# Moving most of the cosine similarities, and the first batch's load of them, out of the handover between the two parts of a one-core decoder kernel

## The reference, cut to what matters

```
sim = stack([cos(embedding, emb_l), cos(embedding, embedding), cos(embedding, emb_r)], axis=1)   # [B, 3, D]
att = repeat(sim, C, axis=1)                  # [B, 3*C, D]
out = einsum('bit,oi->bot', inp_unf * att, w_flat)
```

## Time and profile before

| what | value |
|---|---|
| median of 3 runs | 1395.09 us (1395.02 to 1397.9) |
| the profiled execution's own time | 1392.16 us |
| its span, first to last instruction | 1390.1 us |
| mean granted TensorE clock | 0.992 of full |
| TensorE busy | 1355.7 us, 98% of the span |
| VectorE, ACT, POOL busy | 79%, 67%, 70% |

### The profile page before, as it was taken

The page is one execution under the profiler, slowest core; times in us unless marked ns, Lnnn a source line. Parts: engine busy times, 40 slices in busy tenths (PEclk is TensorE's granted clock), DMA queues, the critical chain, the costliest instruction groups (busy, mean ns, idle before and its releaser), DMA issues. The chain is left out here.

```text
span 1390.1 us, 32350 instructions
## 1 busy us (share of the span) xinstructions
PE 1355.7 (98%) x8306; PEld 1056.5 (76%) x8306; DVE 1095.9 (79%) x3873; ACT 927.2 (67%) x3262; POOL 979.0 (70%) x932
## 2 busy tenths in 40 slices
PE   8999999999999999999986999999999999999996
PEld 6777777777777777777764788888888888888884
DVE  6877787878778777878785688878887788877877
ACT  5887878878888887878785455545554455545544
POOL 4877777777777776777775677667776677767762
PEclk9999999999999999999998999999999999999999
DMA  7354545445453545445468866676665766666652
GB/s 266 100 160 116 159 116 161 121 146 149 121 161 115 165 115 152 132 134 159 131 201 242 185 159 166 157 174 153 161 156 164 172 152 165 156 169 157 161 122 76
DMA packets 109005, 213.03 MB, mean 153 GB/s; under 512 B 26656, under 2 KB 32288, under 8 KB 108960
## 3 DMA queue, kind: packets, MB, share of 16 engines
q1 hardware_dynamic: 108336, 211.46, 56.5%
q10 hardware_dynamic: 624, 1.05, 0.2%
HBM read 131.83 MB, written 34.47 MB: 120 GB/s over the span
## 5 line engine op out<-in xcount | busy, mean ns | idle before, releaser
L483 PE MATMUL wo_ps<-weights,halves 128*128 128x512 f32 x2304 | 569.7, 399 | 3.0 <-DVE weights L685 2.9
L483 PEld LDWEIGHTS wo_ps<-weights,halves 128*128 128x128 f32 x2304 | 421.5, 188 | 138.0 <-issue 53.3
L769 ACT ACTIVATE pexp<-sm,smin 128x128 f32<-128x128 f32 x1024 | 398.1, 391 | 100.6 <-DVE smin L622 99.7
L1197 PE MATMUL wo_ps<-weights,halves 128*128 128x512 f32 x1464 | 368.2, 399 | 4.3 <-PEq L145 4.3
L915 POOL TENSOR_TENSOR pn<-pexp,prec 128x512 f32<-128x512 f32 x256 | 266.7, 1047 | 98.5 <-DVE prec L629 98.5
L1667 POOL TENSOR_TENSOR prods<-prod,prods 128x512 fp32r<-128x512 f32 x186 | 251.6, 1360 | 119.9 <-ACT prods L1528 114.9
L1197 PEld LDWEIGHTS wo_ps<-weights,halves 128*128 128x128 f32 x1464 | 270.3, 189 | 62.6 <-issue 5.2
L622 DVE CUSTOM_DVE_ANT_0 sm<-s_ps,mask_t 128x128 f32<-128x128 f32 x1024 | 231.9, 282 | 26.1 <-PE s_ps L513 20.9
L1528 ACT CAST prods<-prod 128x512 fp32r<-128x512 f32 x189 | 117.1, 620 | 181.0 <-DVE prod L1380 146.7
L769 ACT ACTIVATION_READ_ACCUMULATOR pexp<-sm,smin 128x1 f32 x1024 | 193.0, 189 | 0.0
L1380 DVE TENSOR_TENSOR prod<-att,x 128x512 f32<-128x512 f32 x189 | 185.1, 993 | 9.5 <-DMA att<-sim_scratch 7.2
(11 more groups left out here) (130 smaller groups left out, 1645.8 us busy)
## 6 DMA issues: line engine op xcount, KB each, us to landing
att<-sim_scratch SPq DMA_DIRECT2D x192, 252.0 KB
pt<-blocks SPq DMA_DIRECT2D x636, 64.0 KB, 2.0
ctx_t<-in_ctx SPq DMA_DIRECT2D x32, 576.0 KB, 5.1
raw<-in_xT SPq DMA_DIRECT2D x32, 512.0 KB, 3.8
xn<-in_x SPq DMA_DIRECT2D x32, 512.0 KB, 7.6
ot_scratch<-ot SPq DMA_DIRECT2D x63, 256.0 KB, 2.1
raw<-ot_scratch SPq DMA_DIRECT2D x31, 512.0 KB, 6.8
out<-late SPq DMA_DIRECT2D x31, 512.0 KB, 6.2
```

Of the source, the lines that this page charges most:

```text
L483: mm = pe.matmul(qkv_ps[(par + g) % 2][:], xs[:, par, xl, k], w_sb[:, wl, g, k], start=(k == 0 and n == 0), stop=(k == KT - 1 and n == 2))
L769: ins = nc.scalar.activation(pexp[:, c % 2, i * P:(i + 1) * P], sm[:, c % 2, i * P:(i + 1) * P], ACT.Exp, bias=smin[:, c % 2, i:i + 1], sc ...
L1197: mm = pe.matmul(wo_ps[n][:], os_t[:, par, ol, k], wo_sb[:, wl, k, n * BANK:(n + 1) * BANK], start=(k == 0 and m == 0), stop=(k == KT - 1 ...
```

## The change

Similarities of the first 24 batches are made during steps 24 to 29, and only those of the last 8 at the end of part one.

- SP loads the sums of batches 0 to 23 at the start of step 24 (`load_sums(False)`); VectorE applies the limit at position 5 of step 24, ACT takes the root there, VectorE inverts in two halves in steps 25 and 26 and multiplies in steps 27 and 28, and SP stores five transfers of results in step 29. They work in 96 partitions of `att`, which is otherwise idle in part one.
- The sums of batches 24 to 31 take the old way through 32 partitions. Their stores are all issued by SP, and part two waits for them only in step 1 (own row) and step 4 (the others). The unit of the old stores on ACT's queue is gone.
- `start_att` for batch 0 loads all 1024 columns at once, on one semaphore. SP issues it in step 33 right behind the last moves of probabilities, ahead of the store of batch 31's first half and the late stores. `multiply` of batch 0 waits for all of it before its first product; part two's `load_att(0, 1)` is gone.
- Batch 31's first half goes through `ot_first`, the later columns of `xn0`, so its read waits for `added0` and not for an earlier store. Part one does not wait at its end for that store to land; part two does, in step 1, before it loads `x[2]` into `xn0`.
- Batch 0's averages, power and shift (`average_first`, `invert_root_first`) and the high and low parts of the third batch (`high_out(2)`, `low_third_out`, the latter on VectorE and not on POOL) are made at the end of part one.
- TAIL of part one goes from 4 to 10: steps 24 to 29 are unrolled, and the loop covers 4 to 23.

```diff
-    LEAD, TAIL = 4, 4
+    LEAD, TAIL = 4, 10
+    FIRST = 3 * B // 4
+    EARLY = B - 8
...
+    ot_first = xn0[:, BANK:D]
+    def sim_parts(late):
+        rows = slice(4 * FIRST, P) if late else slice(0, 4 * FIRST)
+        flat = nb if late else att[:].rearrange("p k d -> p (k d)")
...
+            if at_step(t, EARLY):
+                load_sums(False)
             if at_step(t, B):
-                load_sums()
+                load_sums(True)
...
             if at_step(t, LAST):
-                store_sims()
-                store_first_half(b)
                 sp.wait_ge(own_out, 16)
                 sp.wait_ge(sim_out, 16 * 6)
-                start_att(sp, att, att_in, sim_dram, 0, 0)
+                start_att(sp, att, att_in[0], sim_dram, 0, 0, D)
+                store_first_half(b)
+                store_sims(True)
...
+            if at_step(t, EARLY + 5):
+                store_sims(False)
...
-        sp.wait_ge(ot_out[0], 16 * B)
         sp.wait_ge(ot_out[1], 16 * (B - 1))
...
+                if at_step(t, EARLY) and p == 5:
+                    bound_sums(False)
+                if at_step(t, EARLY + 1) and p == 5:
+                    invert_norms(False, 0, HALF_QD)
+                if at_step(t, EARLY + 2) and p == 5:
+                    invert_norms(False, HALF_QD, QD + 1)
+                if at_step(t, EARLY + 3) and p == 5:
+                    pair_norms(False)
+                if at_step(t, EARLY + 4) and p == 5:
+                    cosines(False)
...
             if at_step(t, LAST):
-                invert_norms()
-                cosines()
                 add_first(1)
+                average_first()
+                invert_norms(True, 0, HALF_QD)
+                invert_norms(True, HALF_QD, QD + 1)
+                pair_norms(True)
+                cosines(True)
+                low_third_out()
...
                 if p == 7 and at_step(t, LAST):
-                    store_sims()
                     read_ot(b, 0)
                     high_later(9)
                     load_fourth_o()
+                    high_out(2)
+                if p == 5 and at_step(t, EARLY):
+                    take_root(False)
...
             if at_step(t, LAST):
                 low_out(1, 1)
+                invert_root_first()
                 low_later(9)
...
-        load_att(0, 1)
...
             if at_step(t, 4):
-                for u in range(NU):
-                    sp.wait_ge(ot_out[u], 16 * B)
+                sp.wait_ge(ot_out[1], 16 * B)
+                sp.wait_ge(sim_out, 16 * 10)
+            if at_step(t, 1):
+                sp.wait_ge(own_out, 16 * 2)
+                sp.wait_ge(ot_out[0], 16 * B)
...
-            if k == 0:
-                wait(dve, att_in[h], after(t, 64, 64))
+            if m == 0:
+                wait(dve, att_in[0], after(t, 64, 64))
+            elif k == 0:
+                wait(dve, att_in[1], after(t, 64, 0))
```

More of the change, by code:

```diff
@@ L287, in part1 @@
     QD = D // 4
-    sqs, nbs, norm = nb[:, 0:QD + 1], nb[:, QD + 1:2 * QD + 1], nb[:, 2 * QD + 1:3 * QD + 2]
-    own = rot1[:, 0, 0:QD]
-    own_out = sem("own_out")
+    HALF_QD = QD // 2
     right, ot_last = kept
+    ot_first = xn0[:, BANK:D]
+    def sim_parts(late):
+        rows = slice(4 * FIRST, P) if late else slice(0, 4 * FIRST)
+        flat = nb if late else att[:].rearrange("p k d -> p (k d)")
+        sums, mults, norm = (flat[rows, n * (QD + 1):n * (QD + 1) + width]
+                             for n, width in enumerate((QD + 1, QD, QD + 1)))
+        pair = (right[rows, :], xn0[rows, 0:QD]) if late else (
+            flat[rows, 3 * (QD + 1):3 * (QD + 1) + QD], flat[rows, 4 * (QD + 1):4 * (QD + 1) + QD])
+        return sums, mults, norm, *pair
     @block.sync
@@ L368, in load_third_o, with load_sums @@
             sp.dma_start(raw[:, 0], ot_dram[2]).then_inc(o_in[0], 16)
[L370 to L375, removed]
+        def load_sums(late):
+            first, count = (FIRST, B - FIRST) if late else (0, FIRST)
+            sq_sums, nb_sums = sim_parts(late)[0:2]
+            sums = cs_dram[first, 0, 0:1]
+            sp.wait_ge(cs_out, 16 * (B if late else EARLY))
+            sp.wait_ge(summed, B if late else EARLY)
+            for dst, at, width in ((sq_sums, 0, QD + 1), (nb_sums, D, QD)):
                 sp.dma_start(dst, bass.AP(tensor=sums.tensor, offset=sums.offset + at,
-                                          ap=[[2 * D, B], [QD, 4], [1, width]])).then_inc(cs_in, 16)
+                                          ap=[[2 * D, count], [QD, 4], [1, width]])).then_inc(cs_in, 16)
         def store_zeros():
@@ L384, in store_zeros, with store_sims @@
                              allow_slow_non_contiguous=True).then_inc(sim_out, 16)
[L386 to L392, removed]
+        def store_sims(late):
+            first, count = (FIRST, B - FIRST) if late else (0, FIRST)
+            to_right, to_own = sim_parts(late)[3:5]
+            sp.wait_ge(sim_made, 2 * late + 1)
+            for n, shift in ((0, 1), (1, 1), (3, 0), (4, 0)):
+                sp.dma_start(sim_row(sim_dram, n, shift, first, count), to_right).then_inc(sim_out, 16)
+            sp.wait_ge(sim_made, 2 * late + 2)
+            sp.dma_start(sim_row(sim_dram, 2, 0, first, count), to_own).then_inc(own_out, 16)
         sp.dma_start(xraw[:, 0], xT[0]).then_inc(x_in[0], 16)
@@ L683, in _, with cosines @@
+        def cosines(late):
+            sums, mults, _, to_right, to_own = sim_parts(late)
+            dve.wait_ge(cos_step, 4 * late + 3)
+            dve.tensor_tensor(to_right, to_right, mults, ALU.mult).then_inc(sim_made, 1)
+            dve.wait_ge(cos_step, 4 * late + 4)
+            dve.tensor_tensor(to_own, to_own, sums[:, 0:QD], ALU.mult).then_inc(sim_made, 1)
         for n in range(PIECES):
@@ L775, in read_ot @@
             wait(act, pv_done, after(a, NU, u + 1))
-            if not (at_step(a, B - 1) and u == 1):
-                wait(act, ot_out[u], after(a, 16, 0))
-            nc.scalar.copy(ot_last if at_step(a, B - 1) and u == 1 else ot[:, u], pv_ps[:]).then_inc(ot_read, 1)
+            if at_step(a, B - 1):
+                if u == 0:
+                    act.wait_ge(added0, 2)
+                nc.scalar.copy((ot_first, ot_last)[u], pv_ps[:]).then_inc(ot_read, 1)
+                return
+            wait(act, ot_out[u], after(a, 16, 0))
+            nc.scalar.copy(ot[:, u], pv_ps[:]).then_inc(ot_read, 1)
         def move_last_row():
@@ L1439, in step @@
                 low_lt(z)
-            if valid(c):
+            if valid(c) and not at_step(c, 0):
                 average(c, 0)
```

121 lines of the change are left out of this document (70 added, 51 removed).

## The result

The changed kernel is slower: 1400.38 us median of 15 runs (1396.22 to 1402.95), the kernel before 1395.38 (1393.89 to 1397.9) beside it. The ratio is 1.0028, with a 95% interval of 1.0019 to 1.0036; it is not the quotient of the two medians, which is 1.0036. The forecast was 1391.2 us. The time lies above the range (up to 1396.7), on the side that had a chance of 0.13.

A forecast was written before the change was run, and what follows sets the result against it. TensorE, busy 98% of the span, was taken to bound the kernel. Terms -5.07 (handover), +0.81 (step 24) and +0.36 (unrolling) summed to -3.9 us, from the 1395.09 median to 1391.2 us; range 1389.5 to 1396.7.

The forecast's parts named there:

- the load of `att`: Batch 0's full-width load at the handover: 5.2 us from 755.2, complete at 760.4, bounds 760.1 and 765.0.
- the forecast's own first sign of being wrong: At the handover: batch 0's `att` landing over 9 us after its issue.
- -5.07: At the handover: third convolution at 766.05 instead of 771.12, so TensorE 5.07 us earlier there and behind it.
- The rival that `att` costs by bytes: At the handover: `att` lands at 765.0 or later, clock falls, +3.6 us in all, 1398.7 us; chance 0.13.
- The end of part one: Part one ends with ACT's copy at 756.96; TensorE idles 1.45 instead of 4.31 us and keeps its clock.
- Unrolling, predicted +0.36: Steps 24 to 29 leave the hardware loop: 22.30 instead of 22.24 us each, six times 0.06 us.
- Step 24, predicted +0.81: ACT's root and two table loads, 2.98 us against 2.13 idle, delay `kt` and TensorE's transposes by 0.81 us.
- the rival of a double price: In step 24 a switch of tables costs twice the row: 2.6 us more lost, 1393.8 us; chance 0.05.
- Edits costed at nothing: VectorE's and SP's early work in steps 24 to 29, and SP's added waits in part two: 0 us.
- SP's waits in part two: Before loading `x[2]` and batch 1's `att`, until about 762.5; still some 4 us earlier, nobody waits more.
- The chain behind the third convolution: A chain of latencies, 5.68 us to the sixth convolution and 13.24 to the transposes of `x2`, moving as a whole.
- The forecast's rival of two idle times close together: At the handover: idle times of 1.45 and 0.5 us lower the clock, 2.9 us come back, about 1393.5; chance 0.06.

The follow-up runs named there:

- the looped kernel: The changed kernel with TensorE's and POOL's queues kept in the hardware loop over steps 24 to 29: 1396.68 us, ratio 1.0006 to the kernel before.
- The faster kernel: The changed kernel with TensorE's and POOL's queues looped, batch 0's `att` in two halves, SP's five late stores opening part two: 1391.94 us, 0.9982 to the kernel before.

## Why the prediction was wrong

**The step that failed most: the load of `att`.** The sum had 5.2 us, "near the lower end", with an upper bound of 9.8 from twice the bytes. It landed 13.9 us after the first issue and 11.6 after the last, which is the forecast's own first sign of being wrong. The fourth batch's rows, taken to share the engines for 0.5 us, had them nearly alone from 757.1 to 759.4 (0.54 MB at a share of 0.81). From there `att` took 11.6 us, the stores behind it sharing the last of them; even from the start that the sum had set, 4.3 us behind the first issue, it is 9.6. Stretches with little but `att` show 140 GB/s at a DMA share of 0.84, 16 x 0.84 x 4096 / 140000 = 0.39 us a row of 4 KB and engine, twice the 0.20 us of a 2 KB row worked out in the prediction. The full width also has 428 packets fewer on the data queue than the halves (108224 and 108652), and gains nothing by it: from the first issue to the landing of the last part the four kernels with the full width take 13.5 to 14.9 us, and the three with halves in which VectorE waits for the second take 11.2 to 13.8. The price goes by bytes, at 10 GB/s an engine where a load of 4 KB rows had 24. The choice between the ends went by the wrong comparison: a plain load's row was taken as the measure of a broadcast's. The rows at hand could have said otherwise, since a 2 KB row at under half a load's rate shows only that broadcasting is slow, not that its price is per packet. On the engines that take part, the Trainium skill (DMA: Bandwidth & Descriptors, "Why a DMA increments its semaphore by 16 and not by 1") gives 14 of 16 for 42 partitions, a share of 0.875. The two stretches above show 0.89 and 0.84, one on either side, which alone would not decide. The count of packets agrees: 428 is 384 rows more and 44, and 44 is 3 x 14 + 2, one packet for each engine of the four added transfers.

So -5.07 at the third convolution became +1.64. Of these 6.7 us, 5.05 are the landing of `att`, counted from the last matmul of probabilities, and 1.66 the chain behind it (7.31 us from the first product to the third convolution, where the sum had 5.65), most of it the low clock. The rival that `att` costs by bytes had the mechanism and nearly the place (+2.4 there, chance 0.13), but not its low clock: TensorE fell to 0.50 only after the wait, for one convolution (1.65 us instead of 0.97) and the group behind it. That its time, 1398.7, is so near the measured one is luck, as it has no term for what unrolling cost.

**The end of part one.** Predicted 1.45 us idle, from ACT's copy; measured 2.36. SP's queue was costed at 756.0 to 757.3, and the copy's end at 756.96 was taken for the part's. But SP's moves were issued 1.1 us later in the step than before, and five stores of 32 rows took 0.7 us each, as much as with 128 rows. From its last move to its end SP took 6.37 us, the top of the 5.1 to 6.4 that it was costed at; so SP ended last. The kernel with the stores in part two has 1.10 us idle. That the clock stays full was right at 2.36 us.

**Unrolling, predicted +0.36.** Measured 0.21% alone, 2.9 us, and 2.67 us in steps 25 to 30 of the trace. The term was taken from the length of one unrolled step, step 30, which the kernel before unrolls as well; six more of them are a price that the row could not show. No rival had it. As a miss it is smaller than the handover's (2.5 against 6.7 us), but it is what took the time out of the range: looping the two queues brings 1.0028 back to 1.0006, which is 1395.9 us on the median of before, inside.

**Step 24, predicted +0.81.** Right: the wait for `kt` is 0.81 us, the step 23.19 instead of 22.24. ACT's rows there are a table load of 1.28, the root of 0.42 and a load of 1.28 again:

```profile
556.24 1.28 ACT L885 ACT_TABLE_LOAD   x1
557.54 0.42 ACT L885 ACTIVATE att<-att 96x257 f32<-96x257 f32 x1
557.98 1.28 ACT L835 ACT_TABLE_LOAD   x1
559.27 0.40 ACT L835 ACTIVATE pexp<-sm,smin 128x128 f32<-128x128 f32 x1
```

The next operation stands 0.01 to 0.02 us behind each load, and the rival of a double price fell. Of the Trainium skill's two figures (ScalarE: Activation LUTs, "What ACT_TABLE_LOAD costs") the load's 1283 ns agrees, and the drain of 1380 ns does not show here.

**Edits costed at nothing.** VectorE's and SP's early work: right as far as the looped kernel shows, whose steps 25 to 30 are back at 22.24 to 22.30. SP's waits in part two: nobody waited for it, as predicted, but not because it came earlier: `x[2]` was issued at 772.44 and batch 1's `att` at 772.93, where they had been at 763.01 and 766.73, and where the forecast had them 4 us earlier than before.

**The chain behind the third convolution** was forecast to move as a whole: 4.98 us to the sixth and 12.52 to the transposes of `x2`, against 5.68 and 13.24; it moved together to 0.72 us.

**What stays open.** Why TensorE waits for the last moves of probabilities in six of the changed kernels, with `att` behind them or not, and whether ACT's load of the fourth batch has to do with it. Whether the code transfers of TensorE's queue are what slows SP's issues, and how. What decides the clock at the handover. And the worth of step 24's root in time, beyond its 0.8 us in the trace.

## What to carry to other kernels

Moving a load earlier gains only if all that then ends last moves too: here the width of the load, and five stores at a block's end, each hid the other's cost, and only with both edits was the kernel faster than before, by 0.18%. Take the price of a transfer from rows of the same kind (a broadcast from a broadcast, by bytes and by packets) and, where the two bounds give opposite signs, keep the split that lets the consumer start on the first half. Unrolling for the sake of special steps is not free even when the step's own length is unchanged: leave in the loop each engine that has no special step there.

## What the runs showed of the hardware

Unrolling six more steps of TensorE's queue alone adds eight packets of code and costs 0.17% (0.08 to 0.26), and coincides with loads of `x` issued up to 1.2 us late in the step. The same on SP's or ACT's own queue costs nothing that could be measured (1.0004 and 0.9995).

The granted clock did not go by the longest idle time at the handover alone. After 2.36 us of idle time the changed kernel had 1.00. The faster kernel with its queues unrolled again waited 2.01 us, and its clock fell to 0.50 in the matmul of probabilities behind that wait, before the next one of 0.94; the 21 matmuls then took 7.55 us:

```profile
761.09 1.24 PE L552 MATMUL pv_ps<-pt,v_t 128*32 128x512 f32 x8 [2.01 <-DMA pt<-blocks]
763.28 7.55 PE L1283 MATMUL wo_ps<-weights,halves 128*128 128x512 f32 x21 [0.94 <-PEq L150]
```

```profile
761.00:762.00 1.00, 0.91 (x8) 0.16 (x8) 0.00 (x0) 0.00 (x0) 0.00 (x0) 0.93 0.99 240
762.00:763.00 1.00, 0.34 (x4) 0.00 (x0) 0.00 (x0) 0.59 (x1) 0.00 (x0) 0.50 0.97 168
```

The forecast's rival of two idle times close together, which had 0.06, looks like this kernel, but the second idle time came after the fall and can't be its cause. Nor did the low clock cost anything by the measure used above: from the last matmul of probabilities to the transposes of `x2` this kernel takes 24.89 us, 0.20 less than the faster one.
